# A recurrent attention layer with a quantized feed-forward on one core: seven instructions of the weight rounding, the target scaling, the norm and a bias sum change their places

## The reference

```python
def step(S, inp):                       # one chunk of 16 tokens
    qi, ki, vi, ei = inp
    kh = jnp.einsum('bchd,bhde->bche', ki, S)
    target = vi - ki
    mu = jnp.mean(kh, -1, keepdims=True)
    rstd = jax.lax.rsqrt(jnp.var(kh, -1, keepdims=True) + EPS)
    kh_hat = (kh - mu) * rstd
    g = w * kh_hat + b - target
    gw = g * w
    v_new = (gw - jnp.mean(gw, -1, keepdims=True) - kh_hat * jnp.mean(gw * kh_hat, -1, keepdims=True)) * rstd
    A = jnp.einsum('bchd,bshd->bhcs', qi, ki)
    A = jnp.where(tri, A, 0.0) * jnp.transpose(ei, (0, 2, 1))[:, :, None, :]
    qh = jnp.einsum('bchd,bhde->bche', qi, S) - jnp.einsum('bhcs,bshe->bche', A, v_new)
    o = qi + _ln(qh, w, b)
    S = S - jnp.einsum('bchd,bche->bhde', ki * ei[..., None], v_new)
    return (S, o)
```

```python
wq = w.astype(jnp.float8_e4m3fn).astype(x.dtype)
gate = jax.nn.silu(_quantized_matmul(x, gate_w, gate_scale))
up = _quantized_matmul(x, up_w, up_scale)
return _quantized_matmul(gate * up, down_w, down_scale)
```

## Time and profile before

| | us |
|---|---|
| median of 3 runs (lowest, highest) | 845.81 (844.88, 846.83) |
| the profiled execution | 847.05 |
| its span in the profile | 845.3 |
| TensorE matmul busy | 769.8 (91%) |
| VectorE busy | 667.3 (79%) |
| ScalarE busy | 512.6 (61%) |
| GpSimd busy | 479.9 (57%) |
| span of tile 3, from its first bn_stats to the next tile's | 51.8 |
| the same for tile 4 | 53.4 |
| the same for tiles 5 to 14 | 45.9 to 47.9 |

### The profile page before, as it was taken

One profiled execution on the slowest core, in us unless ns is written; L12 is line 12 of the kernel. 1 busy time (PEld: TensorE's weight loads), 2 busy tenths in 40 slices (PEclk: granted clock), 3 DMA queues, 4 the chain that ended last, 5 costly groups with the idle time before them and its releaser, 6 DMA issues.

```text
span 845.3 us, 24475 instructions
## 1 busy us (share of the span) xinstructions
PE 769.8 (91%) x9068; PEld 587.3 (69%) x9068; DVE 667.3 (79%) x2689; ACT 512.6 (61%) x1356; POOL 479.9 (57%) x853
## 2 busy tenths in 40 slices
PE   8877687787898999999999999999999999979996
PEld 4655455555776677777777686776777686767795
DVE  2788987887887888878887888778887888779644
ACT  1797877777687466555556475656556474652332
POOL 5466757575665656465665647565565646447300
PEclk9899997899999999999999999999999999999999
DMA  8112120211210000000100010000100010000000
GB/s 285 28 51 64 40 76 27 68 35 39 64 51 28 2 29 25 20 9 2 52 2 26 2 40 14 27 2 2 52 2 27 2 39 15 2 1 27 26 26 26
DMA packets 16727, 28.58 MB, mean 34 GB/s; under 512 B 3520, under 2 KB 3520, under 8 KB 16608
## 3 DMA queue, kind: packets, MB, share of 16 engines
q1 hardware_dynamic: 16608, 27.02, 10.2%
HBM read 22.82 MB, written 4.19 MB: 32 GB/s over the span
## 4 chain that ended last, share of the span: by engine, by line
PE 63%; DVE 19%; POOL 8%; ACT 4%; issue 4%; SPq 1%; DMA 1%; ACTq 0%; POOLq 0%; DVEq 0%
PE bank L683 19%; PE bank L463 10%; PE bank L718 10%; PE bank L659 5%; PE bank L630 4%; POOL rho L1335 3%; PE bank L477 3%; PE bank L603 3%; PE bank L616 2%; DVE work L1669 2%; PE bank L497 2%; PE bank L638 2%; DVE work L1673 2%; DVE SQ L1685 1%; PE bank L491 1%
## 5 line engine op out<-in xcount | busy, mean ns | idle before, releaser
L1335 POOL TENSOR_TENSOR rho<-sy,cst 128x2 f32<-128x2 f32 x128 | 89.6, 700 | 198.8 <-DVE sy L1642 198.8
L630 PEld LDWEIGHTS bank<-VX,BDkR 128*64 128x64 f32 x1024 | 43.7, 138 | 62.3 <-issue 26.0
L630 PE MATMUL bank<-VX,BDkR 128*64 128x64 f32 x1024 | 56.7, 232 | 31.1 <-DVE VX L1678 30.3
L1039 ACT ACTIVATE qhR<-bank 128x64 f32<-128x64 f32 x128 | 28.5, 223 | 88.3 <-PE bank L638 87.9
L998 ACT ACTIVATE BDkR<-kR,cst 128x128 f32<-128x128 f32 x256 | 81.6, 400 | 0.0
L984 ACT ACTIVATE BDk<-bank 32x256 f32<-32x256 f32 x124 | 46.6, 375 | 57.4 <-DVE kR L1584 48.5
L1685 DVE TENSOR_TENSOR SQ<-SQ,bank 128x128 f32<-128x128 f32 x128 | 36.5, 285 | 52.9 <-PE bank L630 51.3
L1664 DVE SCALAR_TENSOR_TENSOR work<-work,rho,rR 128x32 f32<-128x32 f32 x256 | 53.2, 249 | 27.8 <-POOL rho L1335 26.4
L603 PEld LDWEIGHTS bank<-SQ,BDk 128*64 128x64 f32 x1024 | 46.1, 139 | 41.1 <-issue 38.8
L603 PE MATMUL bank<-SQ,BDk 128*64 128x48 f32 x1024 | 55.3, 228 | 15.9 <-DVE SQ L1685 14.7
L683 PE MATMUL bank<-xh,GW 128*128 128x256 f32 x384 | 64.8, 291 | 3.9 <-DVE xl L1735 3.5
(11 more groups left out here) (194 smaller groups left out, 2167.0 us busy)
## 6 DMA issues: line engine op xcount, KB each, us to landing
xt<-in_x SPq DMA_DIRECT2D x16, 256.0 KB, 2.8
x<-in_x SPq DMA_DIRECT2D x16, 256.0 KB, 2.9
out<-x SPq DMA_DIRECT2D x16, 256.0 KB, 2.0
yb<-in_gate_w SPq DMA_DIRECT2D x12, 256.0 KB, 2.8
yb<-in_up_w SPq DMA_DIRECT2D x12, 256.0 KB, 2.7
yb<-in_down_w SPq DMA_DIRECT2D x12, 256.0 KB, 2.7
Wk<-in_wk SPq DMA_DIRECT2D x1, 1024.0 KB, 8.0
Wv<-in_wv SPq DMA_DIRECT2D x1, 1024.0 KB, 9.9
```

Of the source, the lines that this page charges most:

```text
L630: ins = mm(dS[p, e], bdkr[:, gh, j % 4, p], VX[:, e], start=True, stop=True, skip_group_check=True)
L1335: tt(dst, src, cst[:, C_NH:C_NH + n], ALU.pow).then_inc(*one)
```

## The change

It moves seven things in five tiles; nothing is computed otherwise.

- Tiles 3 and 4, chunk 6, ScalarE: the four target ACTIVATEs (`prep_rT`) go in front of the two of the weight's powers (`from_exponent`), and `prep_th` stays behind both.
- Tiles 3 and 4, VectorE: the `quantize` of that unit goes from the end of chunk 6 to chunk 7, behind `rR` and in front of the state sum.
- Tile 1, VectorE: the `quantize` of chunk 2 goes to the end of chunk 3.
- Tile 3, POOL, chunk 6: the norm's four instructions go from in front of `fl` and beta to behind them. (In tile 1 the condition changes too, but the order stays.)
- The bias sum `qb` of tile 1 leaves POOL in tile 0, chunk 4 and is made by VectorE in tile 1, chunk 0, in front of the state sum (`second_qb`).

```diff
@@ ScalarE, body
-                    from_exponent(t, j)
+                    if j != 6 or early(t + 1) or not prep:
+                        from_exponent(t, j)
...
                         if prep and not early(t + 1):
                             prep_rT(t + 1)
+                            from_exponent(t, 6)
                             prep_th(t + 1)
@@ GpSimd, body
-                    if j == (6 if rounding(t) else 2) and norm and s:
+                    if j == 2 and norm and s and not rounding(t):
                         norm_rs(t + 2)
...
-                    if j == 4 and prep:
+                    if j == 4 and prep and t > 0:
                         after_rows(NC * t + 4)
                         prep_qb(t + 1, o)
...
-                        if norm and not s:
+                        if norm and (not s or rounding(t)):
                             norm_rs(t + 2)
@@ VectorE
+            def second_qb():
+
+                dve.wait_ge(*prep_v.at("qR", 1))
+                dve.wait_ge(*prep_g.at("qb", 0))
+                m = qR[1][:, :].rearrange("p (gh j e) -> p gh j e", gh=2, e=DH)
+                tt(m, m, bR[:, :].rearrange("p (gh e) -> p gh e", gh=2).unsqueeze(2).broadcast_to([P, 2, NC, DH]),
+                   ALU.add).then_inc(*prep_g.one("qb"))
@@ VectorE, body
                     if j == 0 and post:
                         post_qss(t - 1)
+                    if j == 0 and t == 1:
+                        second_qb()
...
                     if j == 7 and prep:
                         prep_rR(t + 1, o)
+                    if j == 7 and t in (3, 4):
+
+                        for u in unit_before(t, 6):
+                            quantize(u)
...
+                    if (t, j) == (1, 3):
+
+                        for u in unit_before(1, 2):
+                            quantize(u)
                     for u in unit_before(t, j):
                         if not pool_free(t, j):
                             shift(u)
-                        quantize(u)
+                        if (t, j) not in ((1, 2), (3, 6), (4, 6)):
+                            quantize(u)
```

## The result

| | before | after |
|---|---|---|
| median, us (lowest, highest) | 845.81 (844.39, 848.99), 9 runs | 851.92 (849.36, 857.65), 9 runs |
| ratio after / before | | 1.0088, 95% interval 1.0068 to 1.0108 |
| the profiled execution / its span | 847.05 / 845.3 | 851.17 / 849.4 |
| mean granted clock of the span, mean over the executions | 0.983 (104, those beside the experiments) | 0.974 (9) |

The change costs 7.4 us by the ratio (5.8 to 9.1); the two medians are 6.1 apart. The forecast was 3.7, and 849.5 for the time; the median of 851.92 is inside its range of 844.9 to 852.4. The last row of the table points to the missing part: 0.009 of 850 us is 7.7 us of TensorE's work at full speed, so some 15 us more at the lower level, which is half of full speed. The forecast had one fall of 3.4 us.

A forecast was written before the change was run, and what follows sets the result against it. PE (91% busy) holds most of the chain, so edits count by PE's arrival at the next tile. Terms 1.2 + 1.4 - 0.15 - 0.15 = +2.3, plus one clock fall 1.4, give +3.7: 849.5 us, range 844.9 to 852.4.

The forecast's parts named there:

- Tile 3's order: Tile 3, chunks 6 and 7: beta 0.20 later, moved quantize held by POOL's shift, state sum and PE's read late; +1.2 us.
- Tile 4's order: Tile 4, chunks 6 and 7: shift, fl and beta 1.38 later, quantize held, PE's tile 5 query read late; +1.4 us.
- The DMA wait: Tile 3, chunk 7: VectorE newly waits 0.4 us for unit 28's load before its exponent; not on the path.
- Tiles 0 and 1: Moved bias sum and unit 9's quantize gain little, as both ends collide or wait; -0.15 and -0.14 us.
- The clock: PE nearly idle near 206.7 to 210.5 and 260.6 to 264.6 lowers the granted clock; one fall adds 1.4 us.
- One fall of the two is likeliest: Ends of tiles 3 and 4: each clock fall about an even chance, so one expected; 1.4 us.
- Rival 2: Both places, in tiles 3 and 4, bring a clock fall; +5.1 us, 850.9 us; chance 20%.
- Where a stretch lies decides: Ends of tiles 3 and 4: a half-busy PE stretch's position decides a clock fall, each about an even chance.
- The rule of the Trainium skill: Clock: only an unbroken idle gap longer than any here lowers it; by it no fall, sum stays +2.3 us.
- Rival 1: No fall of the clock in tiles 3 and 4; +2.3 us, 848.1 us; chance 20%.
- rival 3: Chunk 7 quantizes slip in front of POOL's shifts, not held; tile 3 0.5, tile 4 1.4; +1.6, 847.4 us; chance 12%.
- rival 4: Tiles 3 and 4: chunk front waits for the targets' way, so earlier targets gain; -2.65 us, 843.2 us; chance 13%.

The follow-up runs named there:

- e13: The changed kernel plus six unused matmuls in front of PE's state write in chunk 7 of tiles 3 and 4; +5.4 us over before (ratio 1.0064).
- e12: Kernel before with only tile 4's part, plus six unused matmuls before PE's state write in chunk 7; +1.7 us over before (1.0020).
- e10: Kernel before with tile 3's norm behind beta and the quantizes of units 26 and 34 behind chunk 7's state sum; -0.3 us (0.9997).
- e1: Kernel before with only the parts in tiles 0 and 1 (bias sum on VectorE, unit 9's quantize a chunk later); -0.1 us (0.9999).
- e2: Kernel before with only ScalarE's four targets in front of the powers in tiles 3 and 4, chunk 6; +6.7 us (1.0079).
- e6: Kernel before with only tile 4's part (targets before powers, unit 34's quantize in chunk 7); +4.1 us (1.0048).
- e14: Kernel before with only tile 3's part (targets first, unit 26's quantize in chunk 7, norm behind beta), a repeat run; +5.6 us (1.0066).
- e3: Kernel before with only the quantizes of units 26 and 34 moved to chunk 7, in front of the state sum; -0.8 us (0.9990).
- e4: The changed kernel plus four unused matmuls in front of PE's state write in chunk 7 of tiles 3 and 4; +4.0 us over before (1.0047).
- e9: The changed kernel with ScalarE's powers in front of the targets again in tiles 3 and 4; +0.4 us over before (1.0005).
- e5: Kernel before with only the norm of tile 3, chunk 6 moved behind fl and beta on POOL; -0.3 us (0.9996).
- e15: Kernel before with tile 3's norm behind beta and the parts in tiles 0 and 1, powers first; -1.3 us (0.9985).

## Why the prediction was wrong

By its own steps:

- **Tile 3's order, +1.2**: right in mechanism and nearly in size. Targets in front, shift 1.4 later, the norm out of the way: beta 8.43 us behind chunk 6's bn_stats instead of 8.10 (+0.33, I had 0.20). Quantize held until POOL's shift plus 0.55. With the clock up (e13), chunks 6, 7 and 0 take 23.49 instead of 22.08: +1.4.
- **Tile 4's order, +1.4**: right. Beta +1.50 (I had 1.38), the sum +2.56 (2.3), and chunks 6, 7 and 0 with the clock up (e12) 22.88 instead of 21.33: +1.55.
- **The DMA wait**: it was there, 0.36 us (I had 0.4), and off the path in the changed kernel, as said. In e10, where the sum is earlier, it is 0.60 and ends VectorE's chunk 7.
- **Tiles 0 and 1, -0.3**: each chunk moved as worked out (-1.04 for -1.0, and -1.90 for -1.9 with +1.68 behind it); e1 measured -0.1 (-1.5 to +1.4), and the chunks together -0.4.
- **The clock, +1.4**: the step that failed, in number and in price. "One fall of the two is likeliest" and "that costs PE 0.42 x 3.41 = 1.4 us of work" were both too low. Both places fall in the changed kernel, in e2 and, each for its own tile, in e6 and e14, and each fall lasts 7 us where I had taken 3.4. It costs 2.2 us in tile 4's chunk 0 (8.46 against 6.19 and 6.31 with the clock up) and 2.6 in tile 5's (9.04 against 6.47), 4.8 in all.

The price was read from the wrong row. The window 230.90:234.31 starts before the fall, which runs from 231.47 to 234.88, so a whole one is 1.7 us of PE's work and not 1.4. And in time that one cost only 0.5: chunks 1 to 5 of tile 4 take 32.8 us with it, and 32.3 in the changed kernel and in e1 without it, because the slower work used up a wait of PE behind it: 0.81 us before the write at 233.22 in e1, none in before. PE's row of chunk 0 has no such wait.

Nor does one row give the length. In the first 3.41 us of the two new falls PE was busy for 2.59 and 2.36, with a gap of 0.82 and 1.12 in them. That suggests these gaps as the reason why the clock stayed down, but no run took them away. But before has a fall of 7 us, from 142.72 to 149.55, in whose first half PE was busy throughout; so such gaps are not needed, and what sets the length stays open. The first halves of before's falls at 231.47 (3.4 us long) and 142.72:

```profile
231.47:234.88 3.41, 3.41 (x19) 3.41 (x18) 2.66 (x15) 3.09 (x9) 3.25 (x7) 0.50 0.27 77
...
142.72:146.13 3.41, 3.41 (x58) 3.08 (x58) 2.26 (x12) 2.98 (x9) 3.25 (x5) 0.50 0.25 77
```

With 4.8 in place of 1.4 the sum is 2.3 + 4.8 = 7.1 us; measured were 7.4 (5.8 to 9.1). Rival 2 (both falls) had the mechanism, and with 1.4 each it too stopped at +5.1. The trace of before would have warned of the length: it has falls of 7 us at 30.1 and at 142.7, where I looked at one of 3.4 only. "Where a stretch lies decides" had no row behind it then; e12 and e13, and the stretches of e3 and e4, fit it. The rule of the Trainium skill that I set against the falls (TensorE: Matmul & The Clock Gate, HAM oscillation: only an unbroken idle gap longer than any here) does not hold in this trace: the longest gap in the changed kernel's two places is 2.04 us, and the clock fell both times.

Rival 1 (no fall) is refuted by the windows, rival 3 (quantizes not held) by the 1.34 and 1.35 us, and rival 4 (the targets' way bounds the chunk) by e2, in which the targets were earlier and chunk 6 was 1.5 us longer.

## What to carry to other kernels

A delay on an engine that only feeds TensorE can cost twice when it makes TensorE stand still in front of its busiest row: once as the wait, and again as half speed on what follows, here 3.0 us of the one and 4.8 of the other. Before pricing a fall of the clock, list every fall in the trace with its length and with what ran beneath it, and take the price where the falls to be expected would lie, on a row that is all PE. And look at what a moved instruction meets in its new place: in front of the state sum the quantize was held by GpSimd and took e9's gain, and behind it (e10) it still carried its load of 2.7 us with it.

## What the runs showed of the hardware

- The granted clock fell behind stretches of 3.4 us in which PE was busy for 1.39 and 1.36 us, with single gaps of 2.04 us at most. It held over stretches with 1.28 (e3) and 1.14 us (e4) of PE work.
- A fall of 3.4 us cost 0.5 us where PE had waits behind it (tile 4, chunks 1 to 5) and 1.5 us in front of a row that is all PE (tile 5's chunk 0 in e13, 7.99 against 6.47); one of 7 us cost 2.2 to 2.8 there.
- The same PE rows at the same place kept the clock in one execution (e12) and lost it in another (e13). Executions of one kernel differ by this: those of e4 go from 844.93 us at a mean clock of 0.987 to 853.37 at 0.969. A difference of 1 us can't be seen through that in twelve runs, as e5 and e15 show.
- A VectorE tensor_tensor with two SBUF inputs beside a POOL tensor_tensor took 1.34, 1.35, 1.23 and 1.15 us instead of 0.68, and ended 0.55 us behind POOL's in the first.
